# A transformer layer stack on one core: token attention by row tile, transposes behind each exponential, and another order of the work

## The reference

```python
x = x + _L0_attn_a_ref(_layernorm(x), norm_weight, w_qkv, temperature, w_out)       # A: attention over channels
x = x + _L0_ffn_ref(_layernorm(x), router_w, actor_w1, ..., gate_w, up_w, down_w)   # F: experts
x = x + _L0_attn_b_ref(_layernorm(x), W_qkv, b_qkv, W_proj, b_proj)                 # B: attention over tokens
x = x + _L0_ffn_ref(_layernorm(x), router_w, actor_w1, ..., gate_w, up_w, down_w)   # F again

# B, for each item of 512 tokens:
attn = einsum('bsd,btd->bst', q, k) * SCALE
xn = sigmoid(attn)
mult = where(xn > .95, 2.0, where(xn > .85, 1.5, where(xn < .1, .1, where(xn < .25, .3, 1.0))))
out = einsum('bst,btd->bsd', softmax(attn * mult), v) @ W_proj + b_proj

# F, for each item: 8 experts of 336 hidden columns; a token takes its k best experts, k from a small actor network
for e in range(8):
    out = out + scores[..., e] * (silu(x @ gate_w[e].T) * (x @ up_w[e].T)) @ down_w[e].T
```

## Time and profile before

| | |
|---|---|
| median of 3 runs | 533.03 us (529.68 to 537.04) |
| profiled execution | 532.75 us, of which 531.0 us from the first to the last instruction |
| granted TensorE clock, mean | 0.99 |
| busy PE, DVE, ACT, POOL | 93%, 66%, 45%, 55% |
| first chunk starts, last chunk starts | 25.68 us, 520.79 us |
| table loads of ScalarE | 40, of 1283 ns each |
| DMA after the first tenth of the span | near nothing |

### The profile page before, as it was taken

How to read it: one execution, slowest core, us unless ns; L and a number is a source line. 1 busy time by engine, 2 the same in 40 slices (tenths; PEclk the granted TensorE clock), 3 DMA queues, 4 the chain that set the end, 5 groups by cost and what they waited for, 6 DMA issues and landing times.

```text
span 531.0 us, 6553 instructions
## 1 busy us (share of the span) xinstructions
PE 495.8 (93%) x2128; PEld 349.3 (66%) x2128; DVE 348.6 (66%) x769; ACT 239.2 (45%) x399; POOL 291.2 (55%) x280
## 2 busy tenths in 40 slices
PE   6797989999996997998989999899998999999996
PEld 6665756776664665766757777577775677666663
DVE  3649483775699797568785699956989354653332
ACT  3386326246622735423836248462383523523221
POOL 4346794238578092734565357553564544655553
PEclk9999999999999998999999999989999899999999
DMA  8600000000000000000000000000000000000000
GB/s 248 200 0 2 0 2 0 1 0 2 1 0 1 0 1 1 0 2 0 2 0 1 0 0 2 0 1 1 21 1 0 1 21 0 1 2 20 0 1 20
DMA packets 7917, 7.38 MB, mean 14 GB/s; under 512 B 716, under 2 KB 7756, under 8 KB 7884
## 3 DMA queue, kind: packets, MB, share of 16 engines
q1 hardware_dynamic: 7884, 6.97, 4.3%
HBM read 5.91 MB, written 1.05 MB: 13 GB/s over the span
## 4 chain that ended last, share of the span: by engine, by line
PE 63%; DVE 16%; issue 4%; ACT 2%; POOL 1%; DVEq 0%; POOLq 0%; ACTq 0%
PE bank L1085 20%; PE bank L949 12%; PE bank L951 11%; PE bank L950 11%; PE bank L1136 3%; DVE t L883 2%; DVE xn L735 2%; PE bank L1124 1%; DVE mk L909 1%; PE bank L1053 1%; DVE mk L908 1%; DVE mk L913 1%; DVE gt L843 1%; DVE mk L912 1%; DVE ge L837 1%
## 5 line engine op out<-in xcount | busy, mean ns | idle before, releaser
L530 POOL TENSOR_TENSOR t<-t,sl 128x512 f32<-128x512 f32 x105 | 136.3, 1303 | 123.0 <-DVE t L883 120.5
L633 ACT ACTIVATE sl<-bank 128x512 f32<-128x512 f32 x168 | 99.9, 597 | 182.8 <-PE bank L951 147.6
L1085 PE MATMUL bank<-t,WD 128*128 128x512 f32 x336 | 168.1, 595 | 0.8 <-ACT YT L639 0.8
L883 DVE TENSOR_TENSOR t<-bank,sbc 128x512 f32<-128x512 f32 x105 | 71.9, 685 | 77.0 <-PE bank L951 76.8
L949 PE MATMUL bank<-xhF,WGh 128*128 128x512 f32 x168 | 100.5, 598 | 2.7 <-ACT sl L633 2.0
L530 POOL TENSOR_TENSOR t<-t,sbc 128x512 f32<-128x512 f32 x63 | 81.6, 1326 | 6.0 <-ACT sbc L627 5.9
L1085 PEld LDWEIGHTS bank<-t,WD 128*128 128x128 f32 x336 | 63.7, 190 | 27.8 <-issue 13.8
L949 PE MATMUL bank<-xhF,WUh 128*128 128x512 f32 x168 | 68.4, 407 | 7.7 <-DVE t L883 7.7
L883 DVE TENSOR_TENSOR t<-bank,sl 128x512 f32<-128x512 f32 x63 | 42.7, 684 | 43.7 <-ACT sl L633 25.8
L951 PE MATMUL bank<-xhF,WUl 128*128 128x512 f32 x168 | 67.1, 399 | 0.0
L951 PE MATMUL bank<-xhF,WGl 128*128 128x512 f32 x168 | 67.0, 399 | 0.0
(11 more groups left out here) (180 smaller groups left out, 688.3 us busy)
## 6 DMA issues: line engine op xcount, KB each, us to landing
stage<-in_gate SPq DMA_DIRECT2D x7, 192.0 KB, 6.1
stage<-in_up SPq DMA_DIRECT2D x7, 192.0 KB, 6.3
WD<-in_down SPq DMA_DIRECT2D x7, 192.0 KB, 6.2
X<-in_x SPq DMA_DIRECT2D x4, 256.0 KB, 5.5
out<-X SPq DMA_DIRECT2D x4, 256.0 KB, 2.3
raw<-in_small SPq DMA_DIRECT2D x1, 388.0 KB, 4.6
raw<-in_small SPq DMA_DIRECT2D x1, 192.0 KB, 2.7
rows<-in_row SPq DMA_DIRECT2D x1, 136.0 KB
```

Of the source, the lines that this page charges most:

```text
L530: pool.tensor_tensor(t2[k % NT2][:, :], t2[k % NT2][:, :], by[:, :], ALU.mult).then_inc(a_done, 1)
L633: act.activation(sl[k % NSL][:, :], bank[k % 2][:, :], ACT.Silu).then_inc(silu_done, 1)
L883: dve.tensor_tensor(t2[k % NT2][:, :], bank[2 + k % 2][:, :], by[:, :], ALU.mult).then_inc(t2_done, 1)
L1085: pe.matmul(OACC[:, :], WD[:, c, :], t2[k % NT2][:, :], start=(c == 0), stop=(c == CH - 1))\
```

## The change

It has five parts.

1. `bpT` i now takes row tile i and transposes its four column tiles, so it needs only exponential i. Its copy writes a strided piece of `PT`. Scores of tile i of the next item wait only for `bpT` i.
2. Each exponential has its own step in the table, each followed some three chunks later by its transposes. Row sums `brs` are double, and their reciprocal moves from `bpT` to `bo`.
3. In `bsp` the first two masks are combined by one scalar-tensor-tensor pass ((m0 + 1) max m1), part 2 only adds masks, and part 3 multiplies the scores and takes the row maximum in one instruction (`tensor_tensor_reduce`); a one-column instruction negates it.
4. `ROUTED_LATE` by batch goes. A set `routed_last`, filled by the planner, says for each chunk whether VectorE takes silu (when the scores are not there or GpSimd is behind) or the scores. It has chunks 0 to 86 and 105 to 111. `sl` has 3 buffers, t 20. A new batch starts as soon as its split input is there.
5. The step tables A, B and F and the cost of `bsp` (.9 to 1.35) are new; F1 has no table of its own.

```diff
-NSL, NT2 = 2, 16
+NSL, NT2 = 3, 20
...
-B_STEPS = [(0, "stats"), (2, "xn"), (4, "xT"), (4, "xl"), (6, "bqk", 0), (7, "bqk", 1), (7, "bqkl", 0),
...
+B_STEPS = [(0, "stats"), (2, "xn"), (5, "xT"), (6, "xl"), (8, "bqk", 0), (9, "bqk", 1), (9, "bqkl", 0),
...
-F_STEPS = [(0, "stats"), (1, "xn"), (3, "xT"), (4, "xl"), (6, "route"), (7, "rexp"), (7, "inner", 0),
-           (10, "inner", 1), (9, "rsum"), (12, "rrank"), (12, "tanh"), (12, "gelu"), (14, "act"),
-           (14, "actk"), (18, "sbc")]
+F_STEPS = [(0, "stats"), (1, "xn"), (4, "xT"), (5, "xl"), (7, "route"), (8, "rexp"), (8, "inner", 0),
+           (10, "rsum"), (11, "inner", 1), (12, "rrank"), (13, "tanh"), (14, "gelu"), (16, "act"),
+           (17, "actk"), (20, "sbc")]
...
     if kind == "bexp":
-        return [("byx", prev), ("bsp", b, s[-1], 3)]
+        return [("bexp", prev, NT - 1), ("byx", b - 2), ("bsp", b, s[-1], 3)]
+    if kind == "bsp":
+        return [("bsp", prev, NT - 1, 3)]
     if kind == "bpT":
-        return [("byx", prev)] + [("bexp", b, i) for i in range(NT)]
+        return [("byx", prev), ("bexp", b, s[-1])]
+    if kind == "bs":
+        return [("bpT", prev, s[-1])]
...
-        n = (k + 1) // CH
-        if (k + 1) % CH or (("xl", "F", n) if n in ROUTED_LATE else ("sbc", n)) in done:
+        if (k + 1) % CH or ("xl", "F", (k + 1) // CH) in done:
             k += 1
             add(("gu", k))
             assert k < NT2 or ("down", k - NT2) in done
+            if ("sbc", k // CH) not in done or len(um_end) < k:
+                routed_last.add(k)
             add(("uk", k))
...
                     if k >= NSL:
-                        act.wait_ge(t2_done if (k - NSL) // CH in ROUTED_LATE else a_done, k - NSL + 1)
+                        act.wait_ge(t2_done if k - NSL in routed_last else a_done, k - NSL + 1)
...
                     if part == 0:
                         wait_free(dve, turn_of["bs", b, i])
                         dve.tensor_scalar(mk[0][:, :], x_, X10 / 10, 2.0, ALU.is_ge, ALU.mult)
-                        chain(dve.tensor_scalar(mk[1][:, :], x_, X25 / 10, 7.0, ALU.is_ge, ALU.mult))
-                        dve.tensor_tensor(mk[0][:, :], mk[0][:, :], mk[1][:, :], ALU.add).then_inc(mk_ready, 1)
+                        chain(dve.tensor_scalar(mk[1][:, :], x_, X25 / 10, 10.0, ALU.is_ge, ALU.mult))
+                        dve.scalar_tensor_tensor(mk[0][:, :], mk[0][:, :], 1.0, mk[1][:, :], ALU.add, ALU.max)\
+                           .then_inc(mk_ready, 1)
...
-                        chain(dve.tensor_tensor(mk[0][:, :], mk[0][:, :], mk[2][:, :], ALU.add))
-                        dve.scalar_tensor_tensor(x_, mk[0][:, :], 1.0, x_, ALU.add, ALU.mult).then_inc(mk_ready, 1)
+                        dve.tensor_tensor(mk[0][:, :], mk[0][:, :], mk[2][:, :], ALU.add).then_inc(mk_ready, 1)
                     if part == 3:
                         dve.wait_ge(mk_ready, step_no + 3)
-                        dve.tensor_reduce(bmx[:, i:i + 1], x_, AX_X, ALU.max, negate=True).then_inc(sp_ready, 1)
+                        chain(dve.tensor_tensor_reduce(x_, mk[0][:, :], x_, 1.0, -3e38, ALU.mult, ALU.max, bmp[:, i:i + 1]))
+                        dve.tensor_scalar(bmx[:, i:i + 1], bmp[:, i:i + 1], -1.0, None, ALU.mult).then_inc(sp_ready, 1)
...
                 if kind == "bpT":
-                    _, b, j = s
-                    t = turn_of[s]
-                    pe.wait_ge(bexp_done, NT * (b + 1))
+                    _, b, i = s
+                    t = turn_of[s]
+                    pe.wait_ge(bexp_done, NT * b + i + 1)
                     m = turn(t)
-                    for i in range(NT):
-                        r = pe.transpose(m[:, i * P:i * P + P], Sb[:, i, j * P:j * P + P], ident[:, :])
+                    for j in range(NT):
+                        r = pe.transpose(m[:, j * P:j * P + P], Sb[:, i, j * P:j * P + P], ident[:, :])
                     r.then_inc(m_full[t % 3], 1)
```

More of the change, by code:

```diff
@@ L77 @@
 WARM = (12, 2, 4, 7, 10)
[L78 to L81, removed]
+A_STEPS = [(0, "stats"), (1, "xn"), (4, "ag"), (5, "xT"), (6, "ar"), (8, "asim"), (9, "ass"), (10, "ascale"),
+           (12, "asT"), (13, "amax"), (14, "aexp"), (15, "awo"), (17, "am"), (19, "am2"), (21, "y")]
@@ L82 @@
+A1_STEPS = [(2, "asim"), (3, "ass"), (4, "ascale"), (7, "asT"), (8, "amax"), (9, "aexp"), (10, "awo"),
+            (12, "am"), (13, "am2"), (15, "y")]
 F0_STEPS = [(0, "route"), (1, "inner", 0), (2, "rexp"), (3, "inner", 1), (3, "rsum"), (5, "rrank"), (5, "tanh"),
             (6, "gelu"), (8, "act"), (8, "actk"), (11, "sbc")]
-F1_STEPS = [(0, "stats"), (0, "xn"), (3, "xT"), (4, "xl"), (6, "route"), (7, "rexp"), (7, "inner", 0),
-            (9, "inner", 1), (9, "rsum"), (11, "rrank"), (11, "tanh"), (11, "gelu"), (13, "act"),
-            (13, "actk"), (16, "sbc")]
@@ L100 @@
+A_STARTS = (6, 25)
 B_STARTS = (29, 48, 67, 90)
@@ L144, in needs @@
     if kind == "bo":
-        return [("bpT", b, i) for i in range(NT)]
+        return [("bpT", b, NT - 1)]
     if kind == "yT":
@@ L163, in plan @@
     last = CH * 2 * NB
-    threads = [thread("F", n, {0: F0_STEPS, 1: F1_STEPS}.get(n, F_STEPS), CH * n - F_AHEAD if n else 0) for n in range(2 * NB)]
+    threads = [thread("F", n, F_STEPS if n else F0_STEPS, CH * n - F_AHEAD if n else 0) for n in range(2 * NB)]
     threads += [[CH * (n + 1) + 3, [(0, ("yT", n))], 0] for n in range(2 * NB - 1)]
@@ L174, in plan @@
     um_end, downs = [], [0]
+    routed_last = set()
     def ready(s):
@@ L257, in plan @@
     add(("yT", 2 * NB - 1))
-    return steps, order
+    return steps, order, routed_last
 def build(nc, x_d, small_d, gate_d, up_d, down_d, w2_d, cols_d, rows_d, out_d):
-    steps, norm_no = plan()
+    steps, norm_no, routed_last = plan()
     turn_of = {}
@@ L353, in build @@
         bmx = sb("bmx", [P, NT])
-        brs = sb("brs", [P, NT])
+        brs = [sb(f"brs{i}", [P, NT]) for i in range(2)]
+        bmp = sb("bmp", [P, NT])
         bri = sb("bri", [P, NT])
@@ L522, in _ @@
                     pool.wait_ge(t2_done, k + 1)
-                    if n in ROUTED_LATE:
+                    if k in routed_last:
                         if k % CH == 0:
```

40 lines of the change are left out of this document (19 added, 21 removed).

## The result

The changed kernel takes **556.28 us** (median of 4 runs, 554.88 to 557.76) against 535.03 (529.68 to 537.18): ratio 1.041, 95% interval 1.032 to 1.051. The forecast was 516. The profiled execution took 554.88, its span is 553.1. One experiment (e5) met disturbed executions (1003 and 1755 us; one of the kernel before in its group took 1753): its numbers leave them out, and its profile was taken again (e5b).

A forecast was written before the change was run, and what follows sets the result against it. TensorE loses 41.6 us to waits and half clock, VectorE itself bounding chunks 41 to 59. Stretch remainders leave 24.6 lost, 17.0 less: span 531.0 to 514.0, plus 1.75 around it, say 516 us; range 504 to 533.

The forecast's parts named there:

- The silu buffers: Third buffer and VectorE taking silu remove ScalarE's 25.6 us of waiting for GpSimd; PE regains some 2.5 us.
- The falls of the clock at 345 and 411: Sign to look for: TensorE's granted clock no longer falls at these two times, one batch apart.
- chunks 87 to 106: Stretch of the run whose lost time was to fall from 4.8 to 2 us.
- the exponentials' waits: Single exponentials cost PE nothing if row maxima are in time; wrong if ScalarE waits over 1.4 us at each.
- singles as such: 16 single exponentials replace 8 pairs: 56 table loads instead of 40, within 0.8 to 1.4 us slack, costing PE nothing.
- the step on the tables: Later transposes, gelu and actor steps, row tiles over four chunks, cut waits; stretch remainders judged between none and all.
- chunks 107 to 128: Stretch whose lost time was to fall from 4.2 to 2 us.
- 60 to 86: Chunks whose lost time was to fall from 5.7 to 4 us, through buffer and actor's product waits going.
- 0 to 40: Chunks whose lost time was to fall from 13.0 to 10.5 us, as waits for normalized tiles get a chunk more.
- Chunks 41 to 59: Stretch bound by VectorE, whose lost time was to fall from 13.8 to 6 us.
- the rival: Contention with GpSimd's products stays the bound, first two blocks keep 19.5 us of loss: 5.5 saved, 527 us; 28%.
- The rival on the slower side: Exponentials waiting for VectorE's maximum block silu; PE stalls some 2 us at most of 16 places: some 549 us; 12%.

The follow-up runs named there:

- e5: Changed kernel with only the router table's decision copy at step 18 instead of 20, actor's decision at 16 instead of 17: 542.99 and 545.56 us; 543.43 when profiled again.
- e14: Kernel before with only 3 silu buffers and 20 t buffers: 531.08 us, ratio 0.994.
- e9: Changed kernel with each of the 16 exponentials one chunk later: 555.87 us, ratio 1.042.
- e8: Changed kernel with only the transposes and split of the router's input one chunk earlier: 550.03 us, ratio 1.033.
- e11: Changed kernel with both the router's split input and its decision earlier (the edits of e8 and e5): 538.48 us, ratio 1.010.
- e17: e4 with gelu one chunk later and the actor's product and decision two chunks later: 531.08 us, ratio 0.995.
- e1: Changed kernel with the attention of before (step table, paired exponentials, transposes after four, old mask passes): 564.11 us, ratio 1.057.
- e12: Changed kernel with GpSimd's t products over 64 of 512 columns, the rest left without its factor: 519.07 us, ratio 0.971.
- e13: Kernel before with GpSimd's t products over 64 of 512 columns, the rest left without its factor: 509.20 us, ratio 0.953.
- e16: Changed kernel with the old router and actor step tables and the old mask arithmetic, new attention otherwise kept: 539.25 us, ratio 1.013.
- e4: Kernel before with only the product order per chunk, batch start after the split input, 3 silu and 20 t buffers: 530.72 us, ratio 0.993.
- e10: Changed kernel with the old router and actor step tables and each exponential one chunk later: 535.22 us, ratio 1.003.
- e15: e4 with the new mask arithmetic (fused multiply and maximum): 539.59 us, ratio 1.010.
- e3: Changed kernel with the old mask arithmetic (bf16 add, multiply pass, separate maximum): 557.27 us, ratio 1.042.

## Why the prediction was wrong

**Right.** Single durations held: the pass that replaced the first bf16 add 0.693 (said 0.694), the fused pass 0.682 at the median, its negation 0.154, 56 table loads of 1.283; the accumulator read is 0.081, not 0.15 to 0.19. All passes on masks and maxima together, summed over their groups, went from 97.7 us to 102.7. The silu buffers: waits gone, and e14 gives 3.4 us by its ratio (4.5 by the medians) where 2.5 were said. The falls of the clock at 345 and 411 went, though others came at 76.9, 155.4 and 391.0, and chunks 87 to 106 came down, to 3.3 (said 2), by less than a stretch is good to. That the exponentials' waits cost TensorE nothing held: e9 moves 31 us of them away for 0.4 us, which is no difference that can be told. Whether singles as such cost nothing against pairs, as I had it, no run shows by itself.

**Wrong: the step on the tables and the remainders drawn from it.** I read "three chunks behind instead of two" as slack for whoever waits, and set each stretch's remainder by whether VectorE's work fits in the chunks that it has. A step in a list that engines run in order is not given time by a later place; it is put behind other work. Two such places show it, by e5, e8 and e11: the router's split input came to stand behind an addition to X and the fused pass of a row tile as well, with the other mask passes ahead of it in any case, while a score product needed its bank, and the decision came after its batch had begun, so GpSimd got four products at once, just beside those passes. I had the list for that place and asked of it what VectorE had ahead of gelu, not what the bank's turn waited for. The terms: chunks 107 to 128 said 2, measured 14.4 (2.5 with both steps back); 60 to 86 said 4, measured 11.1 (8.6; 5.9 with all old tables); 0 to 40 said 10.5, measured 17.1 (15.2; 14.3).

**Mis-sized: contention.** Chunks 41 to 59, said 6, measured 17.3, and 10.0 (e17) to 26.2 (e1) in every version with GpSimd's full products. I counted VectorE's 43 us of work against PE's 44 "contention included". Without GpSimd's full products the stretch loses 2.3 and 2.8 (e12, e13), so nearly all of it goes with those products, and VectorE's busy time there falls from 68.2 to 44.0 us in e12: contention, as the rival had it (28%), with the backlog that goes with it; but the rival gave it an end at 527, since it left the tables their gains.

**The rival on the slower side** (549, 12%) had nearly the right time by the wrong mechanism, which is luck. The row on which it would be judged came out as it said, exponentials waiting 35.1 us, and I would have taken it for shown had e9 not been run. Its other half, a VectorE late by 3 us and more and another fall of the clock, is what happened; TensorE met it at the t products and at the bank, not behind silu.

**What remains open.** With the old masks the new attention costs 8.5 us against e4 (e16, where I had expected 3 to 6), 4 to 5 of it in chunks 41 to 59. By e10 the waits of the exponentials are at most 2 us of it; which of its steps it is, single exponentials and their 16 more table loads among them, was not tried. That chunks 60 to 86 get worse by the earlier split alone (e8) is not explained, nor are the 4.1 us more in chunks 0 to 40, of which the two steps give back 1.9 (e11).

## What to carry to other kernels

Before a step of an in-order program is moved later "to give it time", write down for each engine what it now stands behind, which buffer or bank it frees and who is next in that one's turn; a chunk of distance counts only if that list stays empty. Price a wait by moving it away, not by its length: 31 us of waiting were worth nothing here, while 0.65 us of lateness at another place went with 3 us more. And where one engine's passes stretch beside another's, first measure how much of the loss is there at all, by shortening one side's operands: here 23 of the 41.6 us lost, where the best kernel tried gained some 4, by its buffers and not by its order.

## What the runs showed of the hardware

A pass of VectorE that takes 0.41 us at the shortest takes 1.48 at the median of its 16 in the kernel after and 0.48 with GpSimd's products cut short (L917). Over the run GpSimd's 168 products of some 1.3 us cost VectorE 55 us of 349 before and 70 of 364 after (e13, e12).

The granted clock of TensorE has two levels in these traces, 2.4 and 1.2 GHz, and the time follows it even where the program is the same: of the executions of the kernel before, one took 529.41 us at a mean clock of 0.996 and one 535.85 at 0.981. At chunk 103 it stayed at 2.4 GHz with 1.99 us idle (e4) and went to 1.2 GHz for 6.8 us behind 2.64 (e15), so the same edit of the masks cost 9 us there and nothing that can be told in e3. The length of the gap does not decide it by itself: in the kernel before it fell behind 1.13 and 0.86 us and stayed behind 3.22.
